# Which engine issues the stack copies of k: SP or GpSimd

## Chip, cores and metric

The kernel runs on one core of a Trainium2 chip. The metric is the device time of one execution in microseconds. The kernel before took 1310.13 us in the median of three runs (1308.75 to 1310.36).

## What is computed

Sixteen sequences of 256 rows with 256 features go through two decoder layers. Cut to what matters here:

```python
x = x + self_attention(layernorm(x))               # 16 heads of 16 features, softmax
x = x + cross_attention(layernorm(x), ctx_768)     # keys and values from 120 context rows, softmax
x = x + linear_int4_and_lora(layernorm(x))
x = x + sigmoid_attention(layernorm(x))            # rms norm, rotary, sigmoid weights / their sum
x = x + cross_attention_one_head(layernorm(x), ctx_768)
x = x + expert_pairs(layernorm(x))                 # two of 64 matrices for each 128 rows
```

The first four lines are one stage of the kernel (`layers_stage`), the last two another (`tail_stage`). The change is in the first, in the two softmax attentions.

## The kernel before, in words

**Units.** `layers_stage` treats one sequence in one of the three attentions as a unit: units 0 to 15 are self attention, 16 to 31 cross attention, 32 to 47 sigmoid attention. A unit's scores are made with bf16 matmuls that keep float32 accuracy: q and k are each split into three bf16 parts (first: the value rounded; second: what is left, rounded; third: what is then left), and six pairs of parts (`PAIRS`) are stacked along the contraction, 16 features of a head each, so one matmul over 96 rows gives the sum of six products.

**Parts.** The projections of q and k are evicted by ScalarE (`projected`, L699) to `l_q` and `l_k`. For softmax units GpSimd makes the first part and the rest (`first_part`, a cast at L572 and a subtraction at L574), ScalarE the second part (`second_part`, L711), GpSimd the third (`third_part`, L580). For the sigmoid units VectorE does what GpSimd does here.

**Stack copies.** Heads lie on partitions in the parts and side by side in the stack, so each stacked block of 16 rows is filled by a DMA of its own from a part: `stack_rows` (L557), twelve for a unit, six for q and six for k. k's first part goes to three blocks, its second to two, its third to one. A copy takes 128 KB, for k in cross units 60 KB. All are issued by SP, in the order of the job list, and each waits for the part it takes (`first_ok`, `second_ok`, `third_ok`). `qstack` and `kstack` have four buffers each (`SLOTS`), and the first copy of a unit waits until the last score group of the unit four before is done. The parts have two buffers, so `first_part` of unit u waits until the copies of unit u-2 have landed. Every copy of q, and every copy of k, adds 16 to one of two semaphores (`stack_dma`, by the parity of the unit), and whoever needs the stack waits for `copies_of(u)`, 96 for each unit so far.

**Order.** One list (`ORDERS`) for each kind of period says in which order all engines go through their jobs; each engine takes from it those that are its own. `LEAD` says for which unit a job in period p is done. The jobs that matter:

- `qa qb ka kb`: projections of unit p+3; `p0q p0k p1q p1k p2q p2k`: its parts; `dq0` to `dk2`: its stack copies (unit p+3 in softmax periods).
- `s`: row maxima of the scores of unit p+2 (TensorE `row_maxima` L941, VectorE L797), sixteen in a self period, eight in a cross one. The first `s` needs the whole stack of the unit, of which the copies were issued in the period before.
- `sT`: transposed scores of unit p (L910) with the maxima as three more contraction rows; `pv`: times the values.
- `np`: parts of the maxima of unit p+1 on GpSimd (L628 to L631); `nT`: their transposition (TensorE L1000, ScalarE L717), which then go to `qstack` by a DMA of ScalarE's.
- `rows`: normalisation of the input rows of unit p+4 (VectorE L785); `vb`: values (L808); `xb`: a bias added on GpSimd (L620); `fac`: the factors of a finished unit (L595, L596).

In a cross period GpSimd's jobs come in the order np, p0q, p0k, p2q, p2k, xb, fac, and SP's in the order dq0, dk0, dq1, dk1, dq2, dk2, cl. From period 26 on, jobs of the linear layer (`fr`, `fxb`, `fz`, `fa`, `fb`, `fst`, `ffac`) stand in the same list.

Of the kernel before, what the change touches and what calls it, by code (L numbers as in the profile page):

```python
# [15 lines left out]
B = 16  # L16
# [402 lines left out]
def layers_stage(nc, t, d):  # L419
# [17 lines left out]
    with ExitStack() as ctx:  # L437
# [34 lines left out]
        n_ok, n_dma = sem("n_ok"), sem("n_dma")  # L472
        cx_dma = [sem(f"cx_dma{i}") for i in range(2)]
        stack_dma = {w: [sem(f"{w}_dma{i}") for i in range(2)] for w in "qk"}

        first_ok = {w: {False: sem(w + "_first"), True: sem(w + "_first_sig")} for w in "qk"}
        rest_ok = {w: {False: sem(w + "_rest"), True: sem(w + "_rest_sig")} for w in "qk"}
# [7 lines left out]
        def width(u):  # L485
            return SC if kind_of(u) == "cross" else S

        def sig(u):
            return kind_of(u) == "sigmoid"

        def nth(u):

            return u - 2 * B + 1 if sig(u) else u + 1

        def copies_of(u):

            return COPY_DMAS * (u // 2 + 1)

        def last_chunk(u):
            return chunk["sT", u, chunks_of(u) - 1]  # L500
# [39 lines left out]
        @block.sync  # L540
        def _(sp):
            def load_context(u):
                if u - 2 >= B:
                    sp.wait_ge(copy_full, copied["cx", u - 2, 0] + 1)
                sp.dma_start(cx[u % 2][:, :], d["ctx"][u - B]).then_inc(cx_dma[u % 2], 16)

            def stack_rows(w, part, u):
                if w + str(part) in ("q0", "k0") and u >= SLOTS:
                    sp.wait_ge(sT_ps, last_chunk(u - SLOTS) + 1)
                ready = second_ok[w] if part == 1 else (first_ok if part == 0 else third_ok)[w][sig(u)]  # L550
                sp.wait_ge(ready, u + 1 if part == 1 else nth(u))
                stack = (qstack if w == "q" else kstack)[u % SLOTS]
                wd = S if w == "q" else width(u)
                for r, pair in enumerate(PAIRS):
                    if pair["qk".index(w)] == part:
                        dst = stack[r * HD:(r + 1) * HD, 0:H * wd].rearrange("c (h x) -> c h x", h=HH)
                        sp.dma_start(dst, parts[w][u % 2][part][:, 0:KT * wd]).then_inc(stack_dma[w][u % 2], 16)  # L557

            for p in PERIODS:
                for job, u, i in ORDER[p]:  # L560
                    if job == "cl":
                        load_context(u)
                    elif job[0] == "d":
                        stack_rows(job[1], int(job[2]), u)

        def first_part(eng, w, u):
            wd = KT * (S if w == "q" else width(u))
            eng.wait_ge(copy_empty, copied[(w + "T" if sig(u) else w + "b"), u, 0] + 1)
            if u >= 2:
                eng.wait_ge(stack_dma[w][u % 2], copies_of(u - 2))  # L570
            src, first = whole[w][:, 0:wd], parts[w][u % 2][0][:, 0:wd]
            eng.tensor_copy(first, src).then_inc(first_ok[w][sig(u)], 1)  # L572
            eng.wait_ge(first_ok[w][sig(u)], nth(u))
            eng.tensor_tensor(src, src, first, ALU.subtract).then_inc(rest_ok[w][sig(u)], 1)  # L574
# [7 lines left out]
        @block.gpsimd  # L582
        def _(pool):
            own, factors_done = [0], [0]

            def link(i):
                own[0] += 1
                i.then_inc(pool_own, 1)
                pool.wait_ge(pool_own, own[0])

            def factors(lo, hi, second_eps):
                f = t["factors"][:, :, lo:hi]
                var = t["mv"][:, 2 * lo:2 * hi].rearrange("p (c two) -> p c two", two=2)[:, :, 1]
                half = t["minus_half"][:, lo:hi]
                link(pool.tensor_scalar(f[:, 3], var, EPS_LN, None, ALU.add))  # L595
                i = pool.tensor_tensor(f[:, 0], f[:, 3], half, ALU.pow)  # L596
                if second_eps is not None:
                    link(i)
                    link(pool.tensor_tensor(f[:, 1], var, f[:, 0], ALU.mult))
                    link(pool.tensor_tensor(f[:, 3], f[:, 1], f[:, 0], ALU.mult))  # L600
                    link(pool.tensor_scalar(f[:, 3], f[:, 3], second_eps, None, ALU.add))
                    link(pool.tensor_tensor(f[:, 1], f[:, 3], half, ALU.pow))
                    i = pool.tensor_tensor(f[:, 2], f[:, 1], f[:, 0], ALU.mult)  # L603
                i.then_inc(factors_ok, hi - lo)

            def after_unit(u):
                pool.wait_ge(stats_ok, stats_no["st", u, 0] + 1)
                cols = batch_cols(u)
                factors(cols.start, cols.stop, None)

            def after_linear(b):
                pool.wait_ge(stats_ok, stats_no["fst", b, 0] + 1)
                cols = batch_cols(b)
                factors(cols.start, cols.stop, EPS_RMS)

            def add_bias(job, u, bias):
                pool.wait_ge(rows_ok, rows_no["fr" if job == "fxb" else "rows", u, 0] + 1)
                for tt in range(TT):
                    x_t = t["x"][:, tile_of(u, tt)]
                    i = pool.tensor_tensor(x_t, x_t, bias[:, :], ALU.add)  # L620
                i.then_inc(xb_ok, 1)

            def maximum_parts(u):
                pool.wait_ge(ring_empty, ring["s", u, maxima_of(u) - 1] + 1)
                if u > 0:
                    pool.wait_ge(copy_full, copied["nT", u - 1, 0] + 1)
                m = nmax[u % 2]
                link(pool.tensor_copy(nparts[:, :, 0, :], m[:, :, :]))  # L628
                link(pool.tensor_tensor(nrest[:, :, :], m[:, :, :], nparts[:, :, 0, :], ALU.subtract))
                link(pool.tensor_copy(nparts[:, :, 1, :], nrest[:, :, :]))  # L630
                pool.tensor_tensor(nparts[:, :, 2, :], nrest[:, :, :], nparts[:, :, 1, :], ALU.subtract).then_inc(n_ok, 1)  # L631

            def rotate(w, u):
                n = u - 2 * B + 1
                pool.wait_ge(tok_ok[w], n)
                pair = lambda a: a[:, :].rearrange("p (x two h) -> p x two h", two=2, h=HH)
                pool.tensor_tensor(pair(tok_sin)[:, :, 0], pair(tok[w])[:, :, 1], pair(t["sin"])[:, :, 0], ALU.mult)
                link(pool.tensor_tensor(pair(tok_sin)[:, :, 1], pair(tok[w])[:, :, 0], pair(t["sin"])[:, :, 1], ALU.mult))
                link(pool.tensor_tensor(tok[w][:, :], tok[w][:, :], t["cos"][:, :], ALU.mult))
                pool.tensor_tensor(tok[w][:, :], tok[w][:, :], tok_sin[:, :], ALU.add).then_inc(rot_ok[w], 1)  # L640
                pool.wait_ge(rot_ok[w], n)

            for p in PERIODS:
                if p in (-4, -3, -2):
                    lo, hi = ((0, 2), (2, 6), (6, B))[p + 4]
                    factors(lo * TT, hi * TT, EPS_LN)
                for job, u, i in ORDER[p]:
                    if job == "np":
                        maximum_parts(u)
                    elif job == "fac":  # L650
                        after_unit(u)
                    elif job == "ffac":
                        after_linear(u)
                    elif job in ("p0q", "p0k") and not sig(u):
                        first_part(pool, job[2], u)
                    elif job in ("p2q", "p2k") and not sig(u):
                        third_part(pool, job[2], u)
                    elif job == "xb":
                        add_bias(job, u, t["bc_l_o" if sig(u) else "bc_x_o"])
                    elif job == "fxb":  # L660
                        add_bias(job, u, t["bc_ffn"])
                    elif job in ("rope_q", "rope_k"):
                        rotate(job[-1], u)
# [216 lines left out]
        def _(pe):  # L880
# [14 lines left out]
            def scores(u, c):  # L895
# [2 lines left out]
                rows_used = STACK if sig(u) else STACK_M  # L898
                if c == 0:
                    for w in "qk":  # L900
                        pe.wait_ge(stack_dma[w][u % 2], copies_of(u))
                    if not sig(u):
                        pe.wait_ge(n_dma, 16 * (u + 1))
                if g >= 2:
# [26 lines left out]
            def row_maxima(u, i):  # L931
                if i == 0:
                    for w in "qk":
                        pe.wait_ge(stack_dma[w][u % 2], copies_of(u))
                out = ring_slot("s", u, i)
                sk = width(u)
                hb = 512 // sk
# [686 lines left out]
```

## Time and profile before

| | |
|---|---|
| median of 3 runs | 1310.13 us |
| profiled execution | 1309.19 us, of which span 1307.4 us |
| TensorE matmuls | 1132.9 us (87%) |
| VectorE | 792.1 us (61%) |
| ScalarE | 638.7 us (49%) |
| GpSimd | 592.1 us (45%) |
| SP's DMA queue (q1) | 46.1% of 16 engines, 96.37 MB |
| ScalarE's DMA queue (q10) | 1.9%, 6.03 MB |
| stack copies of k | 192 of 128 KB, median 4.9 us from issue to landing; 96 of 60 KB, 3.9 us |
| stack copies of q | 288 of 128 KB, 4.3 us |

The span is the profiled execution from first to last instruction. PE is TensorE, PEld its weight loads, DVE VectorE, ACT ScalarE, POOL GpSimd, SPq the DMA issues on SP. "From issue to landing" is counted from the start of the issuing instruction. There is no DMA that GpSimd issues. The layers' stage runs until about 1100 us; self periods last 22.7 us (the cast of q's first part starts at 302.52 and 325.22), cross periods 16.4 us (533.02 and 549.39). In a timeline, "x3" behind a row means that three instructions of the same form stand one behind the other, and the time is theirs together; what stands in brackets is the idle time ahead and what ended it.

### The profile page before, as it was taken

The numbers are of one execution on the slowest core, as the hardware profiler recorded it, in microseconds if no ns is written. First come the engines' busy times: TensorE is split into PE (matmuls) and PEld (weight loads), VectorE is DVE, ScalarE is ACT, GpSimd is POOL, SyncE is SP. The second block draws the span as 40 slices with busy tenths as digits, with TensorE's granted clock in tenths as the row PEclk, the third lists the DMA queues.
The fourth block names the chain that finished last, engine by engine and source line by source line (L and its number), as shares of the span: only waits on it lengthen the run. The fifth ranks groups of instructions, "written<-read, shape, count | busy, mean of one in ns | idle before, by whom it ended". The sixth has DMA issues, their size and how long they took to land. (4 is left out here: it accounts for less than half of the span.)

```text
span 1307.4 us, 24328 instructions
## 1 busy us (share of the span) xinstructions
PE 1132.9 (87%) x8472; PEld 801.5 (61%) x8472; DVE 792.1 (61%) x1785; ACT 638.7 (49%) x1183; POOL 592.1 (45%) x854
## 2 busy tenths in 40 slices
PE   3426799999999999999999889999999997899985
PEld 2214566666666666666666657676766664678753
DVE  2606566666666654555556777878787753356761
ACT  1012455555555565555545335655565674355430
POOL 5063233333324344444446676867676631013343
PEclk8567899999999999999999979999999998899996
DMA  8044656463646545665446174545454570124455
GB/s 246 0 48 71 77 70 79 62 86 51 89 60 81 65 70 68 79 78 79 77 65 74 20 79 61 82 66 85 65 83 65 82 98 1 42 77 128 139 155 177
DMA packets 122502, 103.95 MB, mean 80 GB/s; under 512 B 26615, under 2 KB 122126, under 8 KB 122382
## 3 DMA queue, kind: packets, MB, share of 16 engines
q1 hardware_dynamic: 115502, 96.37, 46.1%
q10 hardware_dynamic: 6880, 6.03, 1.9%
q8 instruction: 69, 1.13, 0.5%
q14 instruction: 51, 0.42, 0.2%
HBM read 28.56 MB, written 4.19 MB: 25 GB/s over the span
## 5 line engine op out<-in xcount | busy, mean ns | idle before, releaser
L673 ACT ACTIVATE l_probs<-l_sT 128x1024 f32<-128x1024 f32 (+1 forms) x320 | 326.7, 1023 | 199.3 <-PE l_sT L910 198.6
L797 DVE TENSOR_REDUCE l_nmax<-l_ring 128x2 f32<-128x512 f32 (+1 forms) x384 | 255.8, 679 | 176.4 <-PE l_ring L941 174.6
L910 PE MATMUL l_sT<-qstack,kstack 99*128 99x256 bf16 (+2 forms) x1280 | 194.1, 274 | 0.0
L926 PE MATMUL l_o<-l_probs,v_heads 128*32 128x256 f32 (+1 forms) x2560 | 178.8, 388 | 0.0
L941 PE MATMUL l_ring<-kstack,qstack 96*128 96x256 bf16 (+1 forms) x1024 | 150.0, 249 | 32.4 <-DMA kstack<-l_kpart 24.0
L910 PEld LDWEIGHTS l_sT<-qstack,kstack 99*128 99x128 bf16 (+2 forms) x1280 | 123.7, 105 | 34.0 <-issue 12.3
L941 PEld LDWEIGHTS l_ring<-kstack,qstack 96*128 96x128 bf16 x1024 | 76.4, 98 | 101.1 <-issue 47.7
L991 PE MATMUL l_ring<-wT,l_zT 128*128 128x256 f32 x512 | 124.3, 385 | 6.7 <-DVE l_nmax L797 5.8
L973 PE MATMUL l_copy<-l_zT,wT 128*128 128x256 f32 x384 | 108.3, 408 | 4.5 <-ACT l_q L699 2.2
L991 PEld LDWEIGHTS l_ring<-wT,l_zT 128*128 128x128 f32 x512 | 91.9, 190 | 27.2 <-issue 8.8
L926 PEld LDWEIGHTS l_o<-l_probs,v_heads 128*32 128x32 f32 (+1 forms) x2560 | 63.6, 109 | 73.1 <-issue 46.7
L1026 PE MATMUL l_ring<-wT,l_attnT 128*128 128x256 f32 x384 | 96.4, 396 | 7.6 <-DVE l_nmax L797 3.6
L785 DVE TENSOR_SCALAR l_z<-x_res,mv,factors 128x256 f32<-128x256 f32 x128 | 89.8, 743 | 11.5 <-POOL factors L603 11.5
L845 DVE TENSOR_TENSOR x_res<-l_ring,x_res 128x512 f32<-128x512 f32 x64 | 44.3, 692 | 86.1 <-PE l_ring L1026 55.2
L1026 PEld LDWEIGHTS l_ring<-wT,l_attnT 128*128 128x128 f32 x384 | 72.1, 198 | 20.0 <-ACT l_zT L681 9.7
L973 PEld LDWEIGHTS l_copy<-l_zT,wT 128*128 128x128 f32 x384 | 69.7, 202 | 16.5 <-ACT l_q L699 7.9
L595 POOL TENSOR_SCALAR factors<-mv 128x2 f32<-128x2 f32 (+2 forms) x67 | 15.0, 224 | 135.5 <-DVE mv L854 121.6
L949 PE MATMUL l_copy<-ident,l_z 128*128 128x128 f32 x256 | 42.5, 291 | 35.9 <-DVE l_z L785 20.3
L628 POOL CAST l_nparts<-l_nmax 128x32 bf16<-128x32 f32 x32 | 6.8, 211 | 134.7 <-DVE l_nmax L797 134.7
L726 ACT ACTIVATE l_o<-l_o 128x512 f32<-128x512 f32 x96 | 57.6, 600 | 15.9 <-PE l_o L926 15.8
L572 POOL CAST l_qpart<-l_q 128x512 bf16<-128x512 f32 x32 | 19.6, 611 | 96.8 <-ACT l_q L699 96.8
L1009 PE MATMUL l_ring<-ident,l_o 128*128 128x128 f32 x384 | 59.3, 277 | 2.7 <-ACT l_o L726 2.4
(196 smaller groups left out, 1983.7 us busy)
## 6 DMA issues: line engine op xcount, KB each, us to landing
qstack<-l_qpart SPq DMA_DIRECT2D x288, 128.0 KB, 4.3
kstack<-l_kpart SPq DMA_DIRECT2D x192, 128.0 KB, 4.9
t_experts<-in_experts SPq DMA_DIRECT2D x60, 256.0 KB, 3.0
kstack<-l_kpart SPq DMA_DIRECT2D x96, 60.0 KB, 3.9
x_res<-in_x ACTq DMA_DIRECT2D x4, 1024.0 KB, 11.7
out_y<-x_res SPq DMA_DIRECT2D x16, 256.0 KB, 3.7
l_cx<-in_ctx SPq DMA_DIRECT2D x16, 90.0 KB, 3.6
t_cx<-in_ctx SPq DMA_DIRECT2D x16, 90.0 KB, 3.2
```

What stands on the lines that cost most here:

```text
L673: act.activation(probs[g % 4][0:kp, :], sT[g % 2][0:kp, :], ACT.Sigmoid if sig(u) else ACT.Exp, scale=HD ** -0.5).then_inc(p_ok, 1)
L726: act.activation(o_sb[half][:, :, :], o_bank[:, :, :], ACT.Identity).then_inc(o_ok, 1)
L785: i = dve.tensor_scalar(z[n % 2][:, tt * D:(tt + 1) * D], t["x"][:, tile_of(u, tt)], t["mv"][:, 2 * c:2 * c + 1], t["factors"][:, which, c ...
L797: dve.tensor_reduce(nmax[u % 2][:, tt, h0:h0 + hb], bank("s", u, i)[:, 0:hb * sk].rearrange("p (h k) -> p h k", h=hb), AX_X, ALU.max, nega ...
L845: dve.tensor_tensor(x_u, bank(job, u)[:, :], x_u, ALU.add).then_inc(ring_empty, 1)
L910: i = pe.matmul(sT[g % 2][0:kp, j * S:(j + 1) * S], kstack[u % SLOTS][0:rows_used, col * width(u) + kt * kp:col * width(u) + (kt + 1) * kp ...
L926: i = pe.matmul(o_bank[32 * j:32 * (j + 1), group % 2, :], v[u % 2][0:kp, kt, 4 * group + j, :], probs[g % 4][0:kp, j * S:(j + 1) * S], st ...
L941: m = pe.matmul(out[:, j * sk:(j + 1) * sk], qstack[u % SLOTS][0:STACK, (h0 + j) * S + tt * P:(h0 + j) * S + (tt + 1) * P], kstack[u % SLO ...
L973: i = pe.matmul(copy_bank[:, mt * wd:(mt + 1) * wd], t["wT"][0:kp, W[kind_of(u)] + "qk".index(w), k, mt * P:(mt + 1) * P], src[0:kp, k, 0: ...
L991: i = pe.matmul(out[0:kq, tt * D:(tt + 1) * D], src[0:kp, k, tt * P:tt * P + kq], t["wT"][0:kp, W[kind_of(u)] + "qkv".index(w), k, :], sta ...
L1009: i = pe.transpose(out[:, (tt * 2 + g) * P:(tt * 2 + g + 1) * P], o_sb[half][:, g, tt * P:(tt + 1) * P], ident[:, :])
L1026: i = pe.matmul(out[:, tt * D:(tt + 1) * D], attnT[:, k, tt * P:(tt + 1) * P], t["wT"][:, W[kind_of(u)] + 3, k, :], start=(k == 0), stop=( ...
```

## The change

For softmax units the copies of k's first part (three) and third part (one) are issued by GpSimd, right behind the instructions that make these parts. They add to semaphores of their own. `stack_landed` waits for both semaphores of k: 32 for each unit whose second part comes from SP and 64 for the four copies of GpSimd, where it was 96. SP still issues q's copies, k's second part, and everything of the sigmoid units.

```diff
+        pool_stack_dma = [sem(f"k_pool_dma{i}") for i in range(2)]
...
+        def stack_landed(eng, w, u):
+
+            if w == "q":
+                eng.wait_ge(stack_dma[w][u % 2], copies_of(u))
+                return
+            soft = min(u // 2 + 1, B)
+            eng.wait_ge(stack_dma[w][u % 2], 32 * soft + COPY_DMAS * (u // 2 + 1 - soft))
+            eng.wait_ge(pool_stack_dma[u % 2], 64 * soft)
...
-                    elif job[0] == "d":
+                    elif job[0] == "d" and (sig(u) or job not in ("dk0", "dk2")):
                         stack_rows(job[1], int(job[2]), u)
...
             if u >= 2:
-                eng.wait_ge(stack_dma[w][u % 2], copies_of(u - 2))
+                stack_landed(eng, w, u - 2)
...
+            def stack_keys(part, u):
+                ready = (first_ok if part == 0 else third_ok)["k"][False]
+                if part == 0 and u >= SLOTS:
+                    pool.wait_ge(sT_ps, last_chunk(u - SLOTS) + 1)
+                pool.wait_ge(ready, nth(u))
+                wd = width(u)
+                for r, pair in enumerate(PAIRS):
+                    if pair[1] == part:
+                        dst = kstack[u % SLOTS][r * HD:(r + 1) * HD, 0:H * wd].rearrange("c (h x) -> c h x", h=HH)
+                        pool.dma_start(dst, parts["k"][u % 2][part][:, 0:KT * wd]).then_inc(pool_stack_dma[u % 2], 16)
...
+                    elif job in ("dk0", "dk2") and not sig(u):
+                        stack_keys(int(job[2]), u)
```

In `scores` and `row_maxima` on TensorE the wait for `copies_of(u)` becomes `stack_landed(pe, w, u)` too.

GpSimd's order in a softmax period is then: np, p0q, p0k, dk0 (three copies), p2q, p2k, dk2 (one copy), then xb and fac. SP's is dq0, dq1, dk1, dq2, cl, in the order of the list.

## Rows read from the trace of the kernel before

**Rows 1.** Windows by stretch: length, busy time of each engine, clock, DMA share, GB/s.

```profile
140.00:520.00 380.00, 360.54 (x3006) 249.37 (x3004) 238.26 (x460) 219.60 (x334) 133.73 (x214) 0.99 0.53 71
520.00:700.00 180.00, 169.02 (x1375) 115.10 (x1374) 105.30 (x226) 96.28 (x182) 89.43 (x161) 1.00 0.57 77
```

**Rows 2.** Waits of all engines, whole span: us in total, times, longest.

```profile
PE l_ring L941 <- DMA kstack<-l_kpart: 24.0, 4, 12.6
```

**Rows 3.** Timeline of SP, first copies of k's first part, cross periods.

```profile
503.21 1.84 SPq L557 DMA_DIRECT2D kstack<-l_kpart  x3
...
668.33 1.83 SPq L557 DMA_DIRECT2D kstack<-l_kpart  x3
...
687.97 1.83 SPq L557 DMA_DIRECT2D kstack<-l_kpart  x3
```

**Rows 4.** Timeline of SP, one cross period and the next one's start.

```profile
535.95 1.83 SPq L557 DMA_DIRECT2D kstack<-l_kpart  x3
537.83 1.29 SPq L557 DMA_DIRECT2D qstack<-l_qpart  x2
...
540.45 0.60 SPq L557 DMA_DIRECT2D qstack<-l_qpart  x1
541.09 0.60 SPq L557 DMA_DIRECT2D kstack<-l_kpart  x1
...
552.32 1.83 SPq L557 DMA_DIRECT2D kstack<-l_kpart  x3
```

**Rows 5.** Landing of k copies: the 541.09 one; 490-720; 140-480; issued 87-92.

```profile
DMA to landing us min/median/max: 4.7/4.7/4.7
...
DMA to landing us min/median/max: 3.3/3.9/5.1
...
DMA to landing us min/median/max: 3.3/4.8/8.5
...
DMA to landing us min/median/max: 5.1/7.0/7.4
```

**Rows 6.** Timeline of TensorE, cross periods.

```profile
546.02 0.38 PE L941 MATMUL l_ring<-kstack,qstack 96*128 96x120 bf16 x4
...
552.05 0.29 PE L1000 MATMUL l_copy<-ident_bf,l_nparts 128*48 128x128 bf16 x2
...
661.70 0.37 PE L941 MATMUL l_ring<-kstack,qstack 96*128 96x120 bf16 x4 [0.41 <-DMA qstack<-l_qpart]
```

**Rows 7.** Timeline of GpSimd, the same cross period.

```profile
536.56 1.16 POOL L580 TENSOR_TENSOR l_qpart<-l_q,l_qpart 128x512 bf16<-128x512 f32 x1
538.40 0.75 POOL L580 TENSOR_TENSOR l_kpart<-l_k,l_kpart 128x240 bf16<-128x240 f32 x1 [0.69 <-ACT l_kpart L711]
539.38 1.42 POOL L620 TENSOR_TENSOR x_res<-x_res,bc_x_o 128x256 f32<-128x256 f32 x2 [0.23 <-DVE l_z L785]
...
545.89 0.21 POOL L628 CAST l_nparts<-l_nmax 128x32 bf16<-128x32 f32 x1 [3.21 <-DVE l_nmax L797]
```

**Rows 8.** Timelines of GpSimd, VectorE and TensorE, one self period.

```profile
307.53 1.16 POOL L580 TENSOR_TENSOR l_qpart<-l_q,l_qpart 128x512 bf16<-128x512 f32 x1
...
309.02 0.73 DVE L785 TENSOR_SCALAR l_z<-x_res,mv,factors 128x256 f32<-128x256 f32 x2
310.63 0.76 DVE L808 TENSOR_TENSOR v_heads<-l_ring,bc_in_v 128x256 f32<-128x256 f32 x2 [0.88 <-PE l_ring L991]
...
321.94 0.38 PE L941 MATMUL l_ring<-kstack,qstack 96*128 96x256 bf16 x2 [0.16 <-DVE l_attn L835]
```

**Rows 9.** Timelines of GpSimd and TensorE, the first unit.

```profile
87.68 1.16 POOL L580 TENSOR_TENSOR l_kpart<-l_k,l_kpart 128x512 bf16<-128x512 f32 x1
...
98.08 0.58 PE L941 MATMUL l_ring<-kstack,qstack 96*128 96x256 bf16 x2 [12.60 <-DMA kstack<-l_kpart]
```

**Rows 10.** Source line L785, 140 to 440 and 840 to 1040: ns min/median/max.

```profile
L785 DVE TENSOR_SCALAR l_z<-x_res,mv,factors x26: 403/406/1349, 150.5 to 422.8; 128x256 f32<-128x256 f32 x26
...
L785 DVE TENSOR_SCALAR l_z<-x_res,mv,factors x36: 761/889/1511, 840.0 to 1033.5; 128x256 f32<-128x256 f32 x36
```

More of the change, by code:

```diff
@@ L900, in scores @@
                     for w in "qk":
-                        pe.wait_ge(stack_dma[w][u % 2], copies_of(u))
+                        stack_landed(pe, w, u)
                     if not sig(u):
@@ L933, in row_maxima @@
                     for w in "qk":
-                        pe.wait_ge(stack_dma[w][u % 2], copies_of(u))
+                        stack_landed(pe, w, u)
                 out = ring_slot("s", u, i)
```

## The prediction

> **What bounds the kernel now.** I read four views: the windows by stretch, to see which engine is full in which stage; the waits, to see whether the stack copies hold anybody; then, because a sum over the whole run hides it, one period of the cross units in the timelines of SP, GpSimd and TensorE side by side; and the landing times of its copies. The windows say TensorE: 360.5 of 380 us in the self stage, 169.0 of 180 us in the cross stage. GpSimd is busy for 133.7 and 89.4 of these, so on average it has room [rows 1]. In the waits, TensorE waited for a k stack copy only four times, 24.0 us in all [rows 2]; these are the first units (12.6 us of it ahead of 98.08 [rows 9]), where the pipeline is not yet filled. So the copies look hidden. The period shows how narrowly.
>
> A cross period of the softmax stage lasts 16.5 us: the first part of k is copied from 503.21 in one period and from 668.33 ten periods later, 165.1 us [rows 3]. In it the kernel makes the parts of unit p+3, and the first row maxima of that unit (L941) stand right behind the first score group of the next period. SP issues twelve copies for a unit, 0.60 us each, ending with k's third part at 541.09 [rows 4]. That one lands 4.7 us later [rows 5], at 545.8. TensorE runs the first maxima of the unit at 546.02 [rows 6]. The slack is 0.2 us. In a later period TensorE already idles 0.41 us for a stack copy (661.70, [rows 6]). So in this stage the chain TensorE, ScalarE, GpSimd parts, copies, landing is as long as TensorE's own work, and what lengthens it is paid once per period.
>
> **The change part by part.** 32 softmax units each lose four copies on SP (three of k's first part, one of its third) and gain them on GpSimd: 128 of the 384 k and q copies of these units. The sigmoid units keep all of theirs on SP.
>
> *On SP.* Four times 0.60 us, 2.4 us per unit, are taken out. Nobody waits for SP as such: its copies of q's second part could start at once when k's first copies no longer stand ahead (537.83 follows on 535.95 plus 1.83 us [rows 4]), but all six copies of k and six of q are needed by the same instruction, and the last one decides. A gain of SP's own is at most the part by which ten periods exceed the 16.37 us seen from 535.95 to 552.32 [rows 4], that is 165.1 less 163.7 = 1.4 us, if all of it came from slow issues on SP. I take 0 and keep 1.4 us as the other end.
>
> *On GpSimd.* No copy is issued by GpSimd in this trace, so its cost c must be bounded. Below: the same copy on SP, 0.60 us [rows 4]. [...] Between the two I take 1.16 us, the row of that engine for that tile. A copy moves each of the tile's 128 rows to a place of its own, so a pass over these rows is the nearest thing the trace has.
>
> The order on GpSimd becomes: first part of q, first part of k, three copies, third part of q, third part of k, one copy. What stands behind the three copies: q's third part, on which SP waits for q's last copy, and k's third part, on which the fourth copy waits; behind that one the bias adds (L620), the factors and next period's maximum parts (L628).
>
> Third parts, cross period [rows 7]. The rest of k is done when q's third part starts, at 536.56. Then 3c, q's third part 1.16, a hand-over of 0.1, k's third part 0.75, a hand-over of 0.1, the fourth copy c. With c = 1.16 that is 536.56 + 3.48 + 2.11 = 542.15, and the issue ends at 543.3, against 541.69 on SP now. Until it lands: the copies now take 3.3 us at least and 4.7 in this place, both counted from the start of a 0.60 us issue [rows 5], so 2.7 to 4.1 us from its end. I take the middle, 3.4, because part of the queue that it now stands in has drained by then but all bytes are the same. Landing 543.3 + 3.4 = 546.7, against 546.02: 0.7 us late per period. With both ends of the landing it is 0 to 1.4 us.
>
> q's last copy: issued at 536.56 + 3.48 + 1.16 + 0.1 = 541.3 instead of 540.45, lands between 3.3 and 4.7 us later, 544.6 to 546.0. It isn't the last.
>
> How often: the cross order of jobs makes parts in thirteen periods. In the last three the linear layer's jobs lengthen the period (19.6 us from 668.33 to 687.97 [rows 3]) while the copies stay where they were, so three microseconds hide the 0.7. Ten periods pay: 7 us.
>
> *The rest of GpSimd in a cross period.* After the fourth copy at 543.3 come two bias adds, 1.42, and the factors, about 1 us: 545.8, and the next maximum parts began at 545.89 [rows 7]. They fit, just. If c were more they would start late, but TensorE transposes them only at 552.05 [rows 6], some five microseconds after they are done, so that costs nothing up to c = 2.
>
> *Self periods* (parts of 16 units and of the first cross ones). q's third part starts at 307.53; 307.53 + 3c + 1.16 + 1.16 + 0.2 + c = 314.7 at c = 1.16. With the longest landing of these units as end (8.5 us [rows 5], less 0.6) 322.6, with 4.1 it is 318.8; TensorE wants the unit at 321.94 [rows 8]. Hidden, except at the worst landing. [...]
>
> *The first units.* TensorE idles for the copies, so here a shift either way counts. Unit 0: k's third part starts at 87.68, moves by 3c to 91.2, ends at 92.3, its copy is issued by 93.5 and lands from 96.2; TensorE starts at 98.08 [rows 9]. The copies then waited in a full queue (7.0 us in the median from issue to landing [rows 5]), and the bytes are unchanged, so I take 0. [...]
>
> *Waits.* TensorE and GpSimd wait for two semaphores of k in place of one, some 110 more waits. The score group ahead of 546.02 waited for three already and TensorE was not idle there; I take 0, and 1 us as the other end.
>
> **Against the rows, two rules.** The Trainium skill ("DMA: Bandwidth & Descriptors", Latency and other measured facts) gives about 1 us to the first byte for a copy issued by GpSimd, which prepares it in software, and about 0.6 us for one of SP's. By that, with 0.4 us more for each of the four copies than SP's 0.60, c would be 1.0 and the fourth copy would land at 545.4 to 546.8, and the sum would be 0 to 8 us, estimated; no run here shows it yet.
>
> The profile shows that GpSimd and VectorE get in each other's way: VectorE's row normalisation (L785) takes 406 ns in the median of the self units and 889 ns in the sigmoid units, where GpSimd computes much of the time [rows 10]. The skill ("SBUF — State Buffer", Who interferes with whom) says why: such a VectorE operation and a GpSimd one hold the same port pair by turns, and descriptor writing of GpSimd counts among these. The rows agree. This speaks against the change, and is the second rival.
>
> **The sum.** Profiled execution 1309.19 us (span 1307.4, 1.8 around it). Plus 10 x 0.7 = 7: 1316.2. The median of the runs, 1310.13, is 0.9 above the profiled one: 1317.
>
> **The rivals.**
>
> *Hidden (1310).* If c is below 1.0, or the landing is short (2.7), the fourth copy lands before 546.02 and nothing is paid. For it: the queue has only a landing's worth left at that time, and c need only be 0.15 us smaller. Against: a slack of 0.2 us before any shift.
>
> *VectorE shut out (1329).* In a self period the three copies are generated from 307.6 to 311.1, and VectorE's normalisation wants to run at 309.02 [rows 8], two instructions. If each waits for the end of a copy (309.9 and 311.1) the pair ends at 311.4 and the value eviction (L808), which began at 310.63, is 0.8 us late; TensorE's ring waits for that directly. Sixteen periods x 0.8 = 13 us; in the cross periods it overlaps the lateness counted above. 1316 + 13 = 1329. It decides if issuing keeps VectorE out for a whole copy. Against: it may do so in short bursts only, and the median of 406 ns in these units [rows 10] shows that today they hardly meet.
>
> [...]
>
> *Faster (1304).* The copies now all share SP's one queue, and in the first units it is full (7.0 us to landing [rows 5], 3.3 at best). If two queues keep the DMA engines better fed, the landing in the first units shrinks to its floor. Three times 1.0 to 1.9 us, 4.5 in all, plus the 1.4 of SP. It decides only where c is below about 0.9, since above that the cross periods take it back. 1310.1 - 5.9 = 1304.
>
> **How the numbers follow.** A difference under 0.2% (2.6 us) can't be told from no change. Chances: late by 0.3 to 1.4 us in each cross period 0.36; VectorE shut out 0.12; costly issue 0.13; hidden 0.25; faster 0.14. Some of the likeliest case (a lateness under 0.26 us) would be within 0.2%; I count that in hidden. So slower 0.61, same 0.25, faster 0.14. The likeliest gives 1317, its own range 1313 to 1325. The whole range reaches below to the hidden case and half of the gain, 1306, and above to 1343, past c = 1.6; about 1 in 10 is left out on each side.
>
> **What would show it.** Copies on GpSimd's queue, with their length c, at the place after L574. k's third part in a cross period 3c later. TensorE's idle time ahead of L941 put down to a k stack copy, about 0.7 us once per cross period, where it had four such waits. A cross period of 17.2 us instead of 16.5, the self period as long as before. For the second rival, L785 above 406 ns in the self units. Wrong would be: a cross period of 16.4 us (hidden), the first wait at 98.08 shorter (faster), or periods longer in the self stage too (costly issue or VectorE).

## The result

The kernel after takes 1313.42 us in the median of 15 runs (1310.53 to 1316.5), the kernel before 1308.43 us in 15 runs on the same chip: ratio 1.0038, 95% interval 1.0029 to 1.0047. That is 5.0 us more. The prediction was 1317.0 us, 6.9 us above the 1310.13 us that stood for the kernel before. The profiled executions lie 7.3 us apart in span (1314.7 to 1307.4), because the one of after is the slowest of its fifteen runs. Three executions of the experiments' kernels took 1397.98, 1657.51 and 2188.46 us, far above the others of the same kernel, and are left out of the ratios.

The page of the profile after, its lines on engines, queues and copies:

```profile
PE 1134.4 (86%) x8472; PEld 802.2 (61%) x8472; DVE 823.7 (63%) x1785; ACT 638.6 (49%) x1183; POOL 659.7 (50%) x982
...
q1 hardware_dynamic: 97070, 84.04, 39.0%
q0 software_dynamic: 5120, 12.33, 7.5%
...
L625 POOL DMA_DIRECT2D kstack<-l_kpart x128 | 70.0, 549 | 12.0 <-POOL l_kpart L590 9.5
...
kstack<-l_kpart POOLq DMA_DIRECT2D x64, 128.0 KB, 6.2
...
kstack<-l_kpart POOLq DMA_DIRECT2D x64, 60.0 KB, 5.4
```

GpSimd's issuing is 128 copies of 549 ns in the mean, 70.0 us, and GpSimd is busier by 67.6 us (659.7, before 592.1). TensorE's work is the same. VectorE is busier by 31.6 us, with no instruction added to it. The lines of the code stand 23 further down than before: the row maxima are L964 now, the normalisation L808, the third part L590, GpSimd's copies L625.

The waits, which answer to [rows 2] (engine, waited for, us in total, times, longest):

```profile
PE l_ring L964 <- DMA kstack<-l_kpart: 27.3, 6, 12.8
```

All of this but 0.3 us is waited in the first units. What is new in the ten cross periods is a wait of TensorE for VectorE's maxima, 3.5 us in nine times, where before had none.

GpSimd's timeline in the cross period that answers to [rows 7], and under it the landing of its single copy of 544.14:

```profile
540.36 1.65 POOL L625 DMA_DIRECT2D kstack<-l_kpart  x3
...
544.14 0.53 POOL L625 DMA_DIRECT2D kstack<-l_kpart  x1 [0.29 <-POOL l_kpart L590]
```

```profile
DMA to landing us min/median/max: 5.6/5.6/5.6
```

SP's end of the same period ([rows 4]) and TensorE's first maxima of the unit ([rows 6]):

```profile
542.17 1.19 SPq L567 DMA_DIRECT2D kstack<-l_kpart  x2
543.40 0.60 SPq L567 DMA_DIRECT2D qstack<-l_qpart  x1
```

```profile
544.62 0.38 PE L964 MATMUL l_ring<-kstack,qstack 96*128 96x120 bf16 x4 [0.39 <-DVE l_nmax L820]
...
550.03 0.37 PE L964 MATMUL l_ring<-kstack,qstack 96*128 96x120 bf16 x4
```

A copy costs GpSimd 0.53 to 0.55 us here, and the last one lands 5.6 us after its start: 549.74, against 550.03 for the maxima. Both numbers differ from the prediction, in opposite directions. Counted from the period's start (GpSimd's cast of q's first part, at 536.84 now and at 533.02 before), this copy is issued at 7.30 us, where SP issued it at 8.07: it leaves 0.8 us earlier than before, and not later.

VectorE's normalisation in a self period and in this cross period, which answer to [rows 8]:

```profile
312.11 2.69 DVE L808 TENSOR_SCALAR l_z<-x_res,mv,factors 128x256 f32<-128x256 f32 x2
314.71 0.74 DVE L831 TENSOR_TENSOR v_heads<-l_ring,bc_in_v 128x256 f32<-128x256 f32 x2
...
542.07 1.93 DVE L808 TENSOR_SCALAR l_z<-x_res,mv,factors 128x256 f32<-128x256 f32 x2
```

The pair of the self period took 0.73 us before [rows 8] and takes 2.69 now; the one of the cross period took 1.13 us before and takes 1.93. From 440 to 700 us one normalisation takes 726 ns in the median and 2074 at most, where it was 409 and 816. VectorE is held up while GpSimd issues.

Where the 7.3 us of the two profiled executions are. The mark for a period is GpSimd's cast of q's first part (in the sigmoid stage, VectorE's).

| stretch | before | after | more |
|---|---|---|---|
| start to the cast of unit 5 | 189.02 | 192.10 | 3.1 |
| a self period | 22.70 | 22.70 | 0 |
| ten cross periods | 164.80 | 166.21 | 1.4 |
| first two sigmoid periods | 45.87 | 47.70 | 1.8 |
| GpSimd's last factors to SP's first copy of the tail stage | 0.97 | 2.34 | 1.4 |

These are 7.7; the rest of the program is 0.4 shorter. Only the third line is what the prediction counted. The last one it did not think of:

```profile
1114.66 0.71 POOL L606 TENSOR_TENSOR factors<-factors,minus_half 128x2 f32<-128x2 f32 x1
```

```profile
1117.71 0.37 SPq L1219 DMA_DIRECT2D t_c_wq<-in_c_wq  x1
```

(GpSimd's and SP's timelines of after; before, the same two begin at 1109.04 and 1110.72.) No work of the program lies between them. At this place each engine ends the stage's block, GpSimd clears the stage's semaphores, and the engines meet. GpSimd ends the block with an instruction called DRAIN, which in the trace begins just ahead of its last operation. It holds the difference (source line L437 on GpSimd, duration in ns; before, then after), and the clearing behind it takes 0.24 and 0.26 us:

```profile
L437 POOLq DRAIN  x1: 817/817/817, 1109.0 to 1109.0; - x1
```

```profile
L437 POOLq DRAIN  x1: 2145/2145/2145, 1114.6 to 1114.6; - x1
```

### The profile page after: what moved, and what is told of

Read it like the earlier page. It is cut to its first block and busy times, and to the rows that moved or that the text cites. A ratio compares the mean times of both kernels' runs of the same rounds, so it can differ in the third digit from the quotient of the medians.

```text
span 1314.7 us, 24376 instructions
## 1 busy us (share of the span) xinstructions
PE 1134.4 (86%) x8472; PEld 802.2 (61%) x8472; DVE 823.7 (63%) x1785; ACT 638.6 (49%) x1183; POOL 659.7 (50%) x982
## 3 DMA queue, kind: packets, MB, share of 16 engines
q0 software_dynamic: 5120, 12.33, 7.5%
q8 instruction: 69, 1.13, 0.5%
## 5 line engine op out<-in xcount | busy, mean ns | idle before, releaser
L964 PE MATMUL l_ring<-kstack,qstack 96*128 96x256 bf16 (+1 forms) x1024 | 150.5, 250 | 38.6 <-DMA kstack<-l_kpart 27.3
L964 PEld LDWEIGHTS l_ring<-kstack,qstack 96*128 96x128 bf16 x1024 | 76.2, 99 | 109.3 <-issue 55.7
L808 DVE TENSOR_SCALAR l_z<-x_res,mv,factors 128x256 f32<-128x256 f32 x128 | 123.1, 1002 | 11.6 <-POOL factors L613 11.6
L625 POOL DMA_DIRECT2D kstack<-l_kpart x128 | 70.0, 549 | 12.0 <-POOL l_kpart L590 9.5
```

The source lines that it names most:

```text
L625: pool.dma_start(dst, parts["k"][u % 2][part][:, 0:KT * wd]).then_inc(pool_stack_dma[u % 2], 16)
L808: i = dve.tensor_scalar(z[n % 2][:, tt * D:(tt + 1) * D], t["x"][:, tile_of(u, tt)], t["mv"][:, 2 * c:2 * c + 1], t["factors"][:, which, c ...
L964: m = pe.matmul(out[:, j * sk:(j + 1) * sk], qstack[u % SLOTS][0:STACK, (h0 + j) * S + tt * P:(h0 + j) * S + (tt + 1) * P], kstack[u % SLO ...
```

## Experiments

Each kernel ran on the same chip as runs of the kernel before, and ratios are to those (their medians are 1308.91 us for the first four kernels, 1310.16 for the next four and 1309.37 for the last four). To judge stretches of single traces one needs their spread: where GpSimd issues nothing, ten cross periods take 163.88 to 164.80 us (four traces), and where GpSimd issues all four copies in them, 165.86 to 166.46 (five).

### Which units pay: the first six, the others

One helper says which copies GpSimd issues, and the three places of the change ask it; the number to wait for is counted from it.

```diff
+        def by_pool(job, u):
+            return job in ("dk0", "dk2") and not sig(u) and (u < 6)     # the other kernel: u >= 6
...
-                    elif job in ("dk0", "dk2") and not sig(u):
+                    elif by_pool(job, u):
                         stack_keys(int(job[2]), u)
```

> GpSimd issues the copies only for units 0 to 5; all later units as in the kernel before. The two profiles put 3.1 us of the change into the first six periods (GpSimd's cast for unit 5 starts 3.1 us later, and then the distance stays) and 1.5 us into the cross periods. Theory A (the first units pay because their stacks land later, cross periods pay on their own): +3 us, 1.0023. Rival B (the loss is spread thinly over all units, and the two profiles' distance in the first periods is chance): 6 of 32 units, +1 us, 1.0007.

1311.99 us, ratio 1.0021 (1.0007 to 1.0034). The cast of unit 5 comes at 193.08 (192.10 in after), the cross periods are as before (164.14 us for ten). But the stage's end takes 2.99 us instead of 0.97, so the first units' own loss is not all of it.

> The complement: GpSimd issues the copies from unit 6 on. Theory A: +1.5 to 2 us, 1.0013, all of it in the cross periods, and self periods of 22.70 us as before, although VectorE's row normalisation takes up to 2.5 us in them. Rival B: +4 us, 1.003. Rival C (VectorE held up costs in self periods too): the self periods are longer than 22.70.

1320.38 us, ratio 1.0080 (1.0062 to 1.0097), slower than the whole change. Ten cross periods take 166.46 us, as in after, self periods 22.70. The stage's end takes 9.53 us. That a part of the change costs more than the whole can't come from its units, nor from its copies one by one: the end of the stage must be a cost of its own, which doesn't simply grow with the copies.

### Which copies pay: the third part's, the first part's

The same helper with `job == "dk2"` (32 copies) and with `job == "dk0"` (96 copies).

> GpSimd issues only the copy of k's third part (one per unit); SP keeps the three of the first part. Nothing then stands between the rest of k and q's third part on GpSimd. Theory D (the delay of GpSimd's third parts by three issues is what makes the last copies late): 0 to +1 us. Theory T (copies issued by GpSimd take longer to land, whenever issued; 5.4 to 6.2 us in the median against 3.9 to 4.9): the third part's copy is the last, so the first units pay nearly in full, +3 us.

1313.13 us, ratio 1.0024 (1.0011 to 1.0038). The cast of unit 5 at 189.43, so nothing is lost at the start. Ten cross periods 165.34. The normalisation of the self periods stays at its 0.40 us: one copy late in the period doesn't meet it. Stage end 3.64. What it expected by the copies' own landing, 3 us more in the first units, didn't come; 2.7 us of its loss are at the stage's end.

> GpSimd issues only the three copies of k's first part; SP keeps the third part's. Theory D: nearly all of the loss, +4 to 5 us. Theory T: these three start early and can land late unseen; +1 to 2 us, mostly by VectorE's hold-up in the cross periods. Theory V (VectorE's normalisation waits for GpSimd's issuing, and that is the cross periods' loss): the cross periods lengthen here, not where GpSimd issues the third part alone.

1319.83 us, ratio 1.0079 (1.0060 to 1.0098). Unit 5 at 191.55, ten cross periods 165.23 with a period of 16.49, and the stage's end 8.87. The normalisation takes 895 ns in the median of the self periods.

This kernel also tells whose landing is late. k's third part is SP's again, and its copy takes just as long: in the period of 536.11 it is issued at 543.31 and takes 5.6 us, where it took 4.7 before. The copies of k by SP in the cross periods, second and third parts (median in us; GpSimd's first parts took 5.5):

```profile
kstack<-l_kpart SPq DMA_DIRECT2D x30, 60.0 KB, 5.6
```

So the longer time to landing isn't a property of the copies that GpSimd issues.

### The delay alone

The kernel before, with two small operations of GpSimd (1.6 us together) at the place of `dk0`. GpSimd issues nothing; it makes q's and k's third parts some 1.6 us later, as behind three copies.

```diff
+                    elif job == "dk0" and not sig(u):
+                        for _ in range(2):
+                            link(pool.tensor_tensor(idle[:, 2:4], idle[:, 0:2], t["minus_half"][:, 0:2], ALU.pow))
```

> The kernel before, all copies on SP, but GpSimd does two powers on 128x2 elements (0.72 us each, result unused) where the change issues the three copies, some 1.6 us, so that q's and k's third parts come as late as in the change. Theory D (delay of the third parts): the first six periods lengthen by 3 us together, cross periods too. Theory T (the copies' own way through the queue): at most +1 us.

1309.45 us, ratio 0.9994 (0.9981 to 1.0006). Cross periods 16.38 (163.99 for ten), stage end 0.96. That the delay costs nothing there proves less than it seems, because it doesn't reach the copies. SP works off its twelve issues one behind the other and comes to k's third part 1.2 us after GpSimd has ended it (at 541.70); the issue, in the period that starts at 534.80:

```profile
542.86 0.60 SPq L558 DMA_DIRECT2D kstack<-l_kpart  x1
```

That is 8.06 us into the period, and before it was 8.07 (541.09, [rows 4], behind the cast at 533.02). So for the cross periods this kernel doesn't test a late copy. In the first units the delay does arrive: TensorE waits 5.73 us for the stack of unit 1, where it waited 4.38 before (for that of unit 0 it was 11.39 us, before 12.60).

```profile
120.17 0.58 PE L946 MATMUL l_ring<-kstack,qstack 96*128 96x256 bf16 x2 [5.73 <-DMA kstack<-l_kpart]
```

The normalisation, 1248 ns in the median of the self periods here, shows that even so long a hold-up of VectorE is hidden in them. In the cross periods TensorE waited 2.8 us for VectorE's maxima, ten times, and their length didn't grow for it.

### VectorE out of the way

In the cross order the normalisation is moved from behind `dk2` to behind `aT s`, where GpSimd issues nothing; once in after, once in before as a control.

```diff
-p2k dk2 rows pv0 s rope_q rope_k
-        sT2 aT s st fst
+p2k dk2 pv0 s rope_q rope_k
+        sT2 aT s rows st fst
```

> The change, with the normalisation of unit p+4's rows (L808, VectorE) three jobs later in the cross order, after TensorE's aT and a maximum, when GpSimd has issued its copies. Theory V (VectorE held up by GpSimd's issuing costs the cross periods): cross periods back to 16.4 from 16.6 us, time 1.5 us under the change. Rival (late landing costs them): no difference.

1315.16 us, ratio 1.0044 (1.0029 to 1.0059). The normalisation is back to 412 ns in the median from 440 to 700 us, and TensorE no longer waits for VectorE's maxima, yet the period is 16.50 (165.86 for ten). Of these ten the last is 17.34: there TensorE waits 1.1 us for the moved normalisation itself. The whole time is not below that of after (1.0044 and 1.0038), as it would have been by the expectation.

> Control: the kernel before with the same later place of the normalisation. Theory V: no difference, since nothing holds VectorE up there. If the later place helps by itself, this one gains as much as the other.

1308.77 us, ratio 0.9994 (0.9982 to 1.0006): the new place by itself does nothing.

### SP's order

In after, SP issues k's second part ahead of q's third in the self periods.

```diff
-sT2 s p2q dq2 nT p1k dk1 sT3
+sT2 s p2q nT p1k dk1 dq2 sT3
```

> The change, with k's second part ahead of q's third in SP's order of the self periods (the cross order has it so already). In the change SP waits there for q's third part, which GpSimd makes only after its three issues, and the two copies of k's second part stand behind it; they were the last to land in the second unit. Theory D: 1 to 2 us under the change, from the first units. Theory T (the DMA engines are full in that stretch whatever the order): no difference.

1313.73 us, ratio 1.0029 (1.0017 to 1.0041). Unit 5 at 190.39 against 192.10. The two intervals overlap, and 1.7 us is also about what kernels that are equal up to this mark differ by at it (189.02 in before, 190.98 in the kernel that changes only later units): inconclusive.

### What the stage's end depends on

By now the gap at the stage's end was 0.97 us with no copies of GpSimd, 2.99 with 24, 3.64 with 32, 8.87 with 96, 9.53 with 104, and 2.34 with 128. The first five lie on 0.97 + 0.082 us for each copy; the last doesn't, unless the count starts anew somewhere between 104 and 128. So two kernels with counts between: the helper with `u < 27` (108 copies) and `u < 29` (116).

> GpSimd issues the four copies for units 0 to 26 only, 108 in all. Between GpSimd's last factor instruction and SP's first copy of the next stage the kernel before takes 0.97 us; with 24, 32, 96 and 104 copies issued by GpSimd so far it took 2.99, 3.64, 8.87 and 9.53, which is 0.97 and 0.082 for each copy, but with all 128 only 2.34. Theory R (the time grows with the position in something that wraps, at 111 to 114 copies): 0.97 + 108 x 0.082 = 9.8 us there, the whole some 11 us above the kernel before (1.0085). Rival S (the number of copies doesn't matter as such; leaving out units or parts does): no telling, but not 9.8 beside 1.3 in the next kernel.

> The same for units 0 to 28, 116 copies, eight more. Theory R: past the wrap, 0.97 + 0.1 to 0.4 = 1.1 to 1.4 us at the stage's end, the whole some 3 to 4 us above the kernel before, and 8 us faster than with 108 copies. A theory in which more copies always cost more gives 10.5 us there.

1321.5 us, ratio 1.0099 (1.0078 to 1.0121), and 1313.71 us, ratio 1.0031 (1.0018 to 1.0044). Eight copies more make the kernel 8 us faster. GpSimd's last factors begin at 1111.41 and 1114.35 and take 0.71 us, SP's first copy of the next stage begins at 1121.98 and 1116.43, so the gap is 9.86 and 1.37 us. GpSimd's DRAIN in the two, first 108 copies:

```profile
L437 POOLq DRAIN  x1: 9660/9660/9660, 1111.4 to 1111.4; - x1
```

```profile
L437 POOLq DRAIN  x1: 1163/1163/1163, 1114.3 to 1114.3; - x1
```

0.97 + 108 x 0.082 = 9.83; and (1.37 - 0.97) / 0.082 = 5 copies for 116, (2.34 - 0.97) / 0.082 = 17 for 128: the same line, begun anew at about 111 copies. All of it is in the DRAIN, which takes 0.82 us with no copy, 2.80, 3.45, 8.68, 9.33 and 9.66 with 24, 32, 96, 104 and 108, and 1.16 and 2.15 with 116 and 128. The last copy of GpSimd was issued at about 717 us, some 400 us earlier, so it doesn't wait for data still on the way.

Then whether it is the copies' number or their size. The kernel before, where GpSimd also issues four copies of 16 rows by 8 bytes in each of 24 periods, 96 in all, into a buffer that nobody reads:

```diff
+                    elif job == "dk2" and u < 24:
+                        if u > 0:
+                            pool.wait_ge(small_dma, 64 * u)
+                        for j in range(4):
+                            pool.dma_start(small[0:16, 2 * j:2 * j + 2], t["ident"][0:16, 0:2]).then_inc(small_dma, 16)
```

> The kernel before, all stack copies on SP, and 96 added copies by GpSimd of 16 rows of 8 bytes into a scratch tile, four for each of units 0 to 23, whose data nobody uses. Theory R1 (the end of the stage costs 0.082 us for each copy GpSimd issued): 0.97 + 7.9 = 8.9 us. Theory R2 (it costs by the rows the copies name, 16 here against 128): about an eighth to a quarter of that, 0.97 + 1 to 2 us. Rival: it is the stack copies' data; then 0.97 us.

1315.18 us, ratio 1.0055 (1.0034 to 1.0076). The gap is 8.85 us, as with 96 large copies (8.87). The DRAIN takes 8.49 us. The line of its page on these copies:

```profile
l_small<-ident POOLq DMA_DIRECT2D x96, 0.1 KB, 6.0
```

So the stage's end goes by the number. The time to landing doesn't come from size either: 0.1 KB needs 6.0 us in the median (6.4 in the self units, 4.7 in the cross ones). In 20 of the 24 units the fourth of them landed within about half a microsecond of the unit's last stack copy: they come through when the burst of copies ends.

### The first part's copies, with VectorE out of the way

The 96 copies of the first part on GpSimd, and the normalisation of the cross periods at its later place.

> GpSimd issues k's first part only (96 copies), and VectorE's normalisation has the later place in the cross order. With GpSimd issuing the first part only the cross periods were 16.49 us against 16.37, and TensorE waited 0.39 us for VectorE's maxima in each. Theory V (that is VectorE's hold-up): 16.37 to 16.39 us here, 1 to 2 us below the 1319.8 of the kernel without the later place. Rival (the first part's copies land late): 16.49. The stage's end costs 8.9 us in both.

1317.65 us, ratio 1.0059 (1.0043 to 1.0074). The cross period is 16.37 again in the median, where it was 16.49 with the normalisation in its old place; VectorE's normalisation, 440 to 700 us, is at 407 ns in the median instead of 742. Over ten periods, which are not all alike, it is 164.80 against 165.23 us, a difference that lies within the spread of equal traces (163.88 to 164.80 is 0.92). The intervals of the two ratios overlap.

## Why the prediction came out as it did

**The sign was right and the total near, but the sum is not the one that was forecast, and that it came near is luck in good part.** Forecast was one term, 10 cross periods x 0.7 us = 7 us. Measured are 5.0 us, in three terms of 1.4 to 2.2: of the forecast's term a fifth to a third came, a second had been put at 0, and a third wasn't thought of.

- *Cross periods, 1.4 us* (164.80 to 166.21 for ten; against the 163.9 that the control and the kernel with the delay show, up to 2.3). The place was right, the size three to five times too large, and the way there was wrong in two steps. The first is the issue. The cost c was taken as 1.16 us; no run shows that figure, and it measured 0.53 to 0.55, below even the lower bound of 0.60. So the last copy left 0.8 us earlier in the period than before, where the forecast had it 1.06 later. The second is the landing. The prediction added 3.4 us (2.7 to 4.1) to the end of the issue, as if the time to landing were the copy's own; it measured 5.6 - 0.53 = 5.1. Two errors cancel for the most part: with the forecast's own start of the third parts and the measured prices, the copy would land at 536.56 + 4 x 0.54 + 2.11 + 5.1 = 545.9, against a deadline of 546.02.

What decides in place of "issue plus latency" can be read from one and the same period in four kernels (us behind its start, the cast of q's first part):

| kernel | start | k's third part issued | landed | first maxima |
|---|---|---|---|---|
| before | 533.02 | 8.07, by SP | 12.8 | 13.00 |
| delay alone | 534.80 | 8.06, by SP | 12.8 | 13.01 |
| first part's copies on GpSimd | 536.11 | 7.20, by SP | 12.8 | 13.12 |
| after | 536.84 | 7.30, by GpSimd | 12.9 | 13.19 |

Over ten cross periods the last stack copy lands 12.7 to 13.0 us behind the start in the median in every kernel, though it is issued anywhere between 7.2 and 9.1 us. Most of this time the DMA engines are full. Seven microseconds of this period before (536.5 to 543.5) and after (540.3 to 547.3), with the DMA engines' mean share as the last number but one (their packets' times overlap, so it can exceed 1):

```profile
536.50:543.50 7.00, 6.66 (x57) 4.53 (x57) 4.86 (x12) 4.95 (x10) 4.33 (x7) 1.00 1.18 122
```

```profile
540.30:547.30 7.00, 6.43 (x56) 4.38 (x56) 5.65 (x12) 4.97 (x10) 6.42 (x11) 1.00 1.16 120
```

A copy that is issued earlier into full engines waits longer, and lands when the burst is through. That is why 5.6 us and 4.7 us are not properties of GpSimd's copies and SP's. What is left is small: in seven of the ten cross periods of after the maxima start the same 0.24 us behind the last landing, which is what being released by it looks like (before, the distance was 0.09 to 0.47). So the forecast's kind of lateness does occur, but in these seven periods the maxima come 0.2 to 0.5 us later behind the start than the usual 13.00, where the forecast had 0.7 in all ten. How much of it is the landing and how much VectorE's hold-up isn't separated: the move of the normalisation takes TensorE's waits for the maxima away and leaves 16.50 us of the 16.58.

The other two terms:

- *The first units, 2.2 us, forecast 0.* In the eight kernels in which GpSimd issues the first part's copies from the start, the cast of unit 5 is at 190.39 to 193.08, mean 192.05; in the six where it doesn't, at 189.02 to 190.98, mean 189.82. The two ranges overlap a little, so the term rests on the means. It is taken up below.
- *The end of the stage, 1.4 us, not thought of.* 0.082 us of GpSimd's DRAIN for each copy that GpSimd has issued, begun anew at about 111. The change with its 128 copies is on the cheap side of that; with 108 of them the kernel was 13 us slower than the one before.

The sum is 5.0; that it meets the measured difference to a tenth is chance, as single traces spread by 0.9 us in the first term and by 2 in the second. Worked out in the same way (ten cross periods less 164.80; 2.2 where the first part's copies of the first units are on GpSimd; the gap at the stage's end less 0.97), the terms give 3.6 us for the first six units alone (measured by the ratio 2.8, interval 0.9 to 4.5), 10.2 for the later units alone (10.5), 3.2 for the third part alone (3.1), 10.5 for the first part alone (10.3), 11.9 for 108 copies (13.0), 3.8 for 116 (4.1), 8.1 for the 96 small ones (7.2), 4.6 for the change with the later normalisation (5.8), 4.8 for the change with SP's other order (3.8), and 10.1 for the first part with the later normalisation (7.7, interval 5.6 to 9.7, the one that misses its interval, by 0.4).

**In the first units** nothing hides a late stack, as the prediction said. Of TensorE's waits for it, that of unit 1 in the timeline of after:

```profile
119.38 0.58 PE L964 MATMUL l_ring<-kstack,qstack 96*128 96x256 bf16 x2 [5.78 <-DMA kstack<-l_kpart]
```

Unit 0's ends at 97.93 and was at 98.08 before [rows 9], so there is no shift, as forecast. Unit 1's was 4.38 us before and is 5.78 now. In the means the loss goes with the first part's copies on GpSimd's queue, but what makes it isn't shown. The third part alone (cast of unit 5 at 189.43) and the small copies (189.69) don't have it. The delay of the third parts can't be excluded: with the delay alone the wait of unit 1 is 5.73 us and the cast comes at 190.77, which is also no more than an equal kernel showed (190.98). Against the delay as the whole cause speaks its ratio, whose interval ends at 1.0006, 0.8 us. In after the last copy to land in unit 1 was one of SP's, 7.2 us after its issue.

**SP's gain** was taken as 0, bound 1.4. No gain in time is to be seen, but the step was misread: SP's four issues did stand in the way of the third parts' copies, which left later than the parts were ready, and with them gone the last copy leaves 0.8 us earlier. Full DMA engines take that back. **The waits** were taken as 0; no run put a price on them by itself.

**The rivals.** *Hidden*: in the self periods it is what happened (22.70 us), in the cross periods almost; the rival fails by the other two terms. Its condition, c below 1.0, held, and its time, 1310, didn't. *VectorE shut out*: the mechanism is real. The pair of normalisations took 2.69 us instead of 0.73, more than the 2.4 that the rival assumed, but the price was 0 in the self periods instead of 16 x 0.8 = 13: the value eviction behind it came 1.0 us later in the period (9.11 us behind the cast instead of 8.11) and TensorE did not run later for it (what it worked on meanwhile was not traced one by one). In the cross periods it may cost something: with the first part's copies alone the median period is 16.49, and 16.37 when the normalisation stands elsewhere, but over ten periods that is 0.4 us, within the spread. With all four copies on GpSimd the same move takes the median from 16.58 to 16.50. The prediction weighed the Trainium skill ("SBUF — State Buffer", Who interferes with whom) here: whoever holds the shared ports first blocks the other. The traces agree as far as VectorE goes: its operation grew from 0.41 to 1.29 us in these cross periods and to 2.52 in the self periods, while GpSimd's issues took 0.53 us in the median and 0.85 at most; a GpSimd that is held up by VectorE is not seen. *Costly issue*: c was half of what was assumed, so nothing of it. *Faster*: the first units lost where this rival had them gain.

**The other rule** that the prediction set beside the rows, the Trainium skill's latencies ("DMA: Bandwidth & Descriptors", Latency and other measured facts: about 1 us to the first byte of GpSimd's copies, 0.6 of SP's), can't be tested here: no run shows a first byte by itself, and the time to landing is set by the burst. The medians of 5.4 and 6.2 us for GpSimd's copies against 3.9 and 4.9 for SP's before are no measure of it, since the latter take in copies of other parts and other moments, and since SP's own copies of k's second part took 5.5 us in the cross periods of after.

**Open.** The first two sigmoid periods took 1.8 us more in the profile of after (47.70 to 45.87), and between 0.2 less and 1.1 more in the other kernels where GpSimd issues copies; the measured sum leaves no room for it in the median, and it isn't explained. Nor is what makes the first units late. Why the DRAIN costs by the copy and starts anew at about 111 isn't shown either: only that it does so between 108 and 116. No kernel that was run is faster than the one before.

## What to carry to other kernels

Moving DMAs to another engine's queue changes three things: that engine's time, the moment at which the copies leave, and what closes the block behind the queue. Before adding a latency to an issue time, look at the DMA engines' share over the whole burst: where they are full, an earlier issue only waits longer, and the landing stays. Look also at the gap at the end of the block, where the number of copies and not their bytes may decide. To price a delay, put it alone into the old kernel, it costs one run; but then check in the trace that the thing you wanted late did leave late, for another engine's queue may hide it. And a part of a change that is slower than the whole points to a cost that isn't in any of its parts.

## What the runs showed of the hardware

- A copy of 128 rows issued by GpSimd kept it for 0.53 us in the median and 0.55 in the mean (0.85 at most), SP for 0.60.
- With the DMA engines at a share of 1.16 to 1.18 for seven microseconds, the last stack copy of a cross unit landed 12.7 to 13.0 us behind the period's start, whether it was issued at 7.2 or at 9.1 us, by SP or by GpSimd. A copy of 16 rows by 8 bytes from GpSimd took 6.0 us in the median beside such bursts, 3.7 at least.
- GpSimd's DRAIN at the end of a stage took 0.82 us with no copy issued by GpSimd and 0.082 us more for each that it had issued, 128 KB and 0.1 KB alike, up to 9.66 us at 108; with 116 it was 1.16 and with 128 it was 2.15.
- A VectorE normalisation of 128x256 float32, 0.40 us alone, took up to 2.5 us beside GpSimd's issuing. Beside GpSimd's two small power operations it took 1.25 us in the median.
- The 12.33 MB that moved to GpSimd's queue took 7.5% of the DMA engines' span there, 99 us; SP's queue fell from 46.1% of 1307.4 us to 39.0% of 1314.7, 90 us less. The same bytes cost the DMA engines about a tenth more.
